# A gated cross-attention and expert-bias block on one core: the batch chain's scratch in PSUM, fewer VectorE operations in it, and mask rows loaded for two units by four transfers

## What is computed

```
x   = x + tanh(g_x) * attn(layernorm(x), ctx)          # x, ctx: (8, 512, 2048), fp32
attn(z, c), per window of 128 columns, 8 heads of 32:
      q = Wq z + bq;  k = Wk z + bk;  v = Wv c + bv    # 512 -> 256
      S = q^T k / sqrt(32), masked;  o = softmax(S) v
      out = (Wo gelu(o) + bo) * mask                   # 256 -> 512
x   = x + tanh(g_f) * ffn(layernorm(x))                # layernorm over the last axis (2048)
ffn(h): logits = h Wr^T + br (64 experts); s = softmax(logits); w = s kept at its 8 largest, else 0
      out = h * sum(w) + w @ expert_bias
```

## Time and profile before

| | |
|---|---|
| median of 3 runs | 1210.87 us (1206.91 to 1213.17) |
| the profiled execution | 1210.61 us, of which span 1208.5 us |
| granted TensorE clock | 0.985 of full speed |

### The profile page before, as it was taken

The page is one execution under the profiler, slowest core; times in us unless marked ns, Lnnn a source line. Parts: engine busy times, 40 slices in busy tenths (PEclk is TensorE's granted clock), DMA queues, the critical chain, the costliest instruction groups (busy, mean ns, idle before and its releaser), DMA issues.

```text
span 1208.5 us, 33324 instructions
## 1 busy us (share of the span) xinstructions
PE 1126.1 (93%) x11661; PEld 1046.1 (87%) x11661; DVE 975.5 (81%) x1882; ACT 1029.2 (85%) x3200; POOL 707.7 (59%) x660
## 2 busy tenths in 40 slices
PE   2699999989999899999999999999999989999977
PEld 2699999889988899898998999988998889989965
DVE  6658878988789777998779887898779977797757
ACT  4688999888989799988998889898998879998954
POOL 2366677466655577466764666746764647746621
PEclk9899999999999999999999999999999989999989
DMA  9267554775548844487556965478554884456433
GB/s 287 74 175 199 143 130 116 237 201 155 132 112 252 218 124 123 117 270 209 131 129 187 235 169 131 119 233 217 141 131 121 253 215 124 125 137 203 110 92 139
DMA packets 169766, 199.82 MB, mean 165 GB/s; under 512 B 27776, under 2 KB 104704, under 8 KB 169472
## 3 DMA queue, kind: packets, MB, share of 16 engines
q1 hardware_dynamic: 168448, 197.20, 59.8%
q10 hardware_dynamic: 1152, 0.50, 0.2%
HBM read 80.06 MB, written 33.65 MB: 94 GB/s over the span
## 4 chain that ended last, share of the span: by engine, by line
PE 56%; SPq 21%; DVE 10%; issue 4%; ACT 4%; DMA 3%; POOL 1%; DVEq 0%; ACTq 0%; POOLq 0%
SPq L521 13%; PE ring L310 7%; PE ring L312 7%; PE ring L311 7%; DVE X L900 4%; PE ring L366 4%; SPq L526 4%; PE ring L325 3%; PE ring L327 3%; PE ring L326 3%; PE ring L349 3%; PE ring L385 3%; PE ring L387 3%; PE ring L386 3%; PE ring L404 3%
## 5 line engine op out<-in xcount | busy, mean ns | idle before, releaser
L615 ACT ACTIVATE P<-ring,nmx 128x128 f32<-128x128 f32 x1024 | 358.6, 402 | 30.9 <-DVE nmx L766 30.3
L310 PE MATMUL ring<-z_hi,wqk_hi 128*128 128x256 f32 x1024 | 299.8, 293 | 24.3 <-DVE z_lo L965 22.0
L311 PE MATMUL ring<-z_hi,wqk_lo 128*128 128x256 f32 x1024 | 292.4, 286 | 0.0
L312 PE MATMUL ring<-z_lo,wqk_hi 128*128 128x256 f32 x1024 | 292.3, 285 | 0.0
L615 ACT ACTIVATION_READ_ACCUMULATOR P<-ring,nmx 128x1 f32 x1024 | 248.5, 243 | 0.0
L1058 POOL TENSOR_TENSOR z_lo<-z,z_hi 128x1024 fp32r<-128x1024 f32 x62 | 147.6, 2381 | 167.5 <-ACT z_hi L583 167.5
L310 PEld LDWEIGHTS ring<-z_hi,wqk_hi 128*128 128x128 f32 x1024 | 198.5, 194 | 37.2 <-DVE wqk_lo L940 21.9
L1070 POOL TENSOR_TENSOR X<-X,xt 128x512 f32<-128x512 f32 x128 | 165.5, 1293 | 67.7 <-DVE xt L801 67.6
L773 DVE STREAM_TRANSPOSE T<-P 128x512 f32<-128x512 f32 x256 | 169.2, 690 | 44.2 <-ACT P L615 24.0
L311 PEld LDWEIGHTS ring<-z_hi,wqk_lo 128*128 128x128 f32 x1024 | 198.9, 194 | 0.0
L312 PEld LDWEIGHTS ring<-z_lo,wqk_hi 128*128 128x128 f32 x1024 | 198.9, 194 | 0.0
(11 more groups left out here) (137 smaller groups left out, 2697.3 us busy)
## 6 DMA issues: line engine op xcount, KB each, us to landing
PT<-T SPq DMA_DIRECT2D x1018, 80.0 KB, 2.1
cx<-in_ctx SPq DMA_DIRECT2D x128, 256.0 KB, 3.9
out_y<-X SPq DMA_DIRECT2D x128, 256.0 KB, 3.1
X<-in_x SPq DMA_DIRECT2D x112, 256.0 KB, 4.6
mg<-in_mask SPq DMA_DIRECT2D x64, 128.0 KB, 3.2
X<-in_x SPq DMA_DIRECT2D x8, 512.0 KB, 8.5
sel<-rows_d SPq DMA_DIRECT2D x256, 3.0 KB
X<-in_eb SPq DMA_DIRECT2D x2, 512.0 KB, 7.7
```

The lines of the kernel that those rows point to most:

```text
L310: e.matmul(o, wqk_hi[:, t, cols], z_hi[:, t, :], t == 0, False)
L311: e.matmul(o, wqk_lo[:, t, cols], z_hi[:, t, :], False, False)
L312: last = e.matmul(o, wqk_hi[:, t, cols], z_lo[:, t, :], False, t == DT - 1)
L615: last = e.activation(P[:, n, :], bank("S", 4 * u + g)[:, k * W:(k + 1) * W], ACT.Exp, bias=nmx[u % 2][:, n:n + 1], accum_out=den[u % 2][: ...
```

## The change

- **Rows.** `load_rows(n)` serves units 2n and 2n+1 by four DMAs, 512 columns each, once; there are two buffers instead of three, and line 341 reads the unit's half twice by an access pattern whose middle step is 0. It is issued where the even unit's was, and waits for the same count of `s_pe`.
- **Batch chain.** The marks (`lr`), the masked exponentials and the sums live in the unused half of LT's PSUM bank (`low(b)`, `wsum`, `gain`); the bank is held until `ac_v` instead of `lg_v`. `c_gate` is gone. `c_scale` has a reduction, two `scalar_tensor_tensor` and a `tensor_scalar` instead of a reduction and three others.
- **Norms.** Adding EPS and negating the mean, before on DVE (823, 824, 926, 927), are on POOL before the power (EPS for norm2; EPS and the mean for the input norm); `norm2` waits for `ac_v` ahead of the aggregation.

```diff
-                take(("LT", b), t, C["c_top"] - C["LT"], lg_v, b + 1)
+                take(("LT", b), t, C["c_sc"] - C["LT"], ac_v, b + 1)
...
-                e.wait_ge(rows_in[u % NRW], 64 * (u // NRW + 1))
+                e.wait_ge(rows_in[u // 2 % NRW], 64 * (u // 2 // NRW + 1))
...
-                    e.matmul(bank("S", 4 * u + g)[:], ones3[head, :], sel[u % NRW][head, :, :].rearrange("p k i -> p (k i)"),
-                             True, False)
+                    e.matmul(bank("S", 4 * u + g)[:], ones3[head, :],
+                             sel[u // 2 % NRW][head, 2 * (u % 2):2 * (u % 2) + 2, :].rearrange("p w i -> p (w i)").unsqueeze(
+                                 1).to_broadcast([32, 2, U]), True, False)
...
-            def load_rows(u):
-                if u >= NRW:
-                    e.wait_ge(s_pe, u - NRW + 1)
+            def load_rows(n):
+                if n >= NRW:
+                    e.wait_ge(s_pe, 2 * (n - NRW + 1))
...
-                    e.dma_start(sel[u % NRW][32 * g + 12:32 * g + 15, :, :].rearrange("k (m w) i -> k m (w i)", m=2),
-                                rows_d[:, 2 * u:2 * u + 2, :].rearrange("k w i -> k (w i)").unsqueeze(1).to_broadcast(
-                                    [3, 2, U])).then_inc(rows_in[u % NRW], 16)
+                    e.dma_start(sel[n % NRW][32 * g + 12:32 * g + 15, :, :], rows_d[:, 4 * n:4 * n + 4, :]).then_inc(
+                        rows_in[n % NRW], 16)
...
-                for u in due(t, C["rows"]):
-                    load_rows(u)
+                for n in due(t, C["rows"], 32, TU // 2):
+                    load_rows(n)
...
             def norm2(b):
                 e.wait_ge(bn2_v, 16 * (b + 1))
+                if b:
+                    e.wait_ge(ac_v, b)
                 for t in range(DT):
                     e.bn_aggr(mv2[:, t, :], bn2[:, t, :, :].rearrange("p a c -> p (a c)")).then_inc(agg2_v, 1)
...
-                e.tensor_scalar(ln2[:, 0, :], mv2[:, :, 0], -1.0, None, ALU.mult).then_inc(neg2_v, 1)
-                e.tensor_scalar(ln2[:, 1, :], mv2[:, :, 1], EPS, None, ALU.add).then_inc(neg2_v, 1)
...
-                e.tensor_scalar(gate[:, 0, :], ln2[:, 2, :], cst[:, TF:TF + 1], None, ALU.mult).then_inc(dm_v, 1)
-                e.wait_ge(dm_v, b + 1)
-                e.tensor_tensor(gate[:, 1, :], gate[:, 0, :], ln2[:, 0, :], ALU.mult).then_inc(gate_v, 1)
...
-                    last = e.match_replace(lr[:, t, :], t8[:, t, :], lg[:, t, :], -3.0e38)
+                    last = e.match_replace(low(b)[:, t, :], t8[:, t, :], lg[:, t, :], -3.0e38)
...
-                e.tensor_tensor(lr[:], lr[:], lg[:], ALU.not_equal).then_inc(sel_v, 1)
+                e.tensor_tensor(low(b), low(b), lg[:], ALU.not_equal).then_inc(sel_v, 1)
+
+            def low(b):
+                return bank("LT", b)[:, DT * NX:2 * DT * NX].rearrange("p (t x) -> p t x", t=DT)
...
-                e.tensor_tensor(ex[:], ex[:], lr[:], ALU.mult).then_inc(wm_v, 1)
+                e.tensor_tensor(low(b), low(b), ex[:], ALU.mult).then_inc(wm_v, 1)
...
-                e.tensor_reduce(sc[:, :, 5:6], w2[:, :, 0, :], AX.X, ALU.add).then_inc(wm_v, 1)
-                e.wait_ge(gate_v, b + 1)
+                wsum, gain = bank("LT", b)[:, 0:DT], bank("LT", b)[:, DT:2 * DT]
+                e.tensor_reduce(wsum, w2[:, :, 0, :], AX.X, ALU.add).then_inc(wm_v, 1)
                 e.wait_ge(wm_v, 4 * b + 3)
-                e.tensor_tensor(sc[:, :, 4:5], sc[:, :, 5:6], gate[:, 0, :].unsqueeze(2), ALU.mult).then_inc(wm_v, 1)
-                e.tensor_tensor(sc[:, :, 7:8], sc[:, :, 5:6], gate[:, 1, :].unsqueeze(2), ALU.mult)
+                e.scalar_tensor_tensor(out=gain, in0=wsum, scalar=cst[:, TF:TF + 1], in1=rs2[:], op0=ALU.mult,
+                                       op1=ALU.mult).then_inc(wm_v, 1)
                 e.wait_ge(wm_v, 4 * b + 4)
-                e.tensor_scalar(sc[:, :, 6:7], sc[:, :, 4:5], 1.0, None, ALU.add).then_inc(ac_v, 1)
+                e.scalar_tensor_tensor(out=sc[:, :, 7], in0=gain, scalar=-1.0, in1=mv2[:, :, 0], op0=ALU.mult, op1=ALU.mult)
+                e.tensor_scalar(sc[:, :, 6], gain, 1.0, None, ALU.add).then_inc(ac_v, 1)
...
             def input_norm(b):
...
+                e.tensor_scalar(rs1[b % 2][:], mv[b % 2][:, :, 1], EPS, None, ALU.add).then_inc(eps1_g, 1)
+                e.tensor_scalar(nm1[b % 2][:], mv[b % 2][:, :, 0], -1.0, None, ALU.mult).then_inc(eps1_g, 1)
+                e.wait_ge(eps1_g, 2 * b + 2)
+                e.tensor_tensor(rs1[b % 2][:], rs1[b % 2][:], half[:], ALU.pow).then_inc(rstd1_g, 1)
```

More of the change, by code:

```diff
@@ L52 @@
     hT=37.5, hT_gap=0.25, ht_hi=41.25, ht_lo=41.75, R=47.25,
-    norm2=27.5, c_gate=33.5, L=36, LT=34, c_top=38.75, c_exp=37.75, c_w=40.75, c_sc=40.75, wT=43, wt_hi=43.25, wt_lo=42.25, mix=43.75, m_gap=0.25,
+    norm2=27.5, L=36, LT=34, c_top=38.75, c_exp=37.75, c_w=40.75, c_sc=40.75, wT=43, wt_hi=43.25, wt_lo=42.25, mix=43.75, m_gap=0.25,
     sx=44.75, sx_gap=1.25, x2=45.25, rl=48.5, rl_gap=2,
@@ L140, in gated_block_kernel @@
         bnst = sb("bnst", [128, DT, 4, 6])
-        mv = sb("mv", [128, DT, 2])
+        mv = [sb(f"mv{i}", [128, DT, 2]) for i in range(2)]
         bn2 = sb("bn2", [128, DT, 4, 6])
         mv2 = sb("mv2", [128, DT, 2])
-        ln1 = [sb(f"ln1_{i}", [128, 3, DT]) for i in range(2)]
-        ln2 = sb("ln2", [128, 3, DT])
+        rs1 = [sb(f"rs1_{i}", [128, DT]) for i in range(2)]
+        nm1 = [sb(f"nm1_{i}", [128, DT]) for i in range(2)]
+        rs2 = sb("rs2", [128, DT])
         L = sb("L", [128, D])
@@ L158, in gated_block_kernel @@
         tab = sb("tab", [128, 2])
-        gate = sb("gate", [128, 2, DT])
         acc = sb("acc", [128, 2])
@@ L196, in gated_block_kernel @@
         out_done = [[sem(f"out{t}{c}") for c in range(4)] for t in range(DT)]
[L197 removed]
+        bn1_v, agg1_v, eps1_g, rstd1_g = (sem(n) for n in ("bn1", "agg1", "eps1", "rstd1"))
         st_a = sem("st")
@@ L203, in gated_block_kernel @@
         gelu_a, othi_a, otlo_g, wo_pe, xt_v, x1_g = (sem(n) for n in ("gelu", "othi", "otlo", "WO", "xt", "x1"))
[L204 to L207 removed]
+        bn2_v, agg2_v, eps2_g, rstd2_g, ht_pe, hthi_a, htlo_v, r_pe = (sem(n) for n in (
+            "bn2", "agg2", "eps2", "rstd2", "hT", "hthi", "htlo", "R"))
+        l_a, lt_pe, lg_v, t8_v, neg_v, mr_v, sel_v, ex_a, w2_v, ac_v = (sem(n) for n in (
+            "L", "LT", "lg", "t8", "neg", "mr", "sel", "ex", "w2", "ac"))
         wm_v, wT_pe, wthi_a, wtlo_v, mix_pe, sx_a, x2_v = (sem(n) for n in (
@@ L1020, in _ @@
                         r_low(u, a)
-                for b in batch(t, C["c_gate"]):
-                    c_gate(b)
                 for b in batch(t, C["c_top"]):
```

56 lines of the change are left out of this document (18 added, 38 removed).

## The result

In the first comparison, four runs each, the changed kernel took 1196.45 us (1194.94 to 1200.85) against 1209.68 (1206.91 to 1213.17): a ratio of 0.9910, 95% interval 0.9883 to 0.9937. In a second one, nine runs against twenty, it was 1198.08 against 1209.15: 0.9924 (0.9896 to 0.9952). The ratios are estimated from all the runs and are not quotients of the medians (here 0.9908). So it is faster by 9 to 11 us. Forecast were 18.3 us and 1192.3; the time lies inside the range of 1186 to 1205, but the gain is little more than half of the forecast one.

What follows compares the result with a forecast made beforehand. TensorE was taken as the bound, losing time to waits and slow clock; 9.1 + 6.8 + 2.2 + 0.4 - 0.2 = 18.3 us off 1210.61 gave 1192.3, range 1188 to 1198, or 1186 to 1205 with two rivals.

Steps and rivals of the forecast that it cites:

- the price of PSUM: Five operations ahead of the division moved to PSUM: 0.3 us per chain or nothing, 0 to 2.1 in all, taken as nothing.
- the start: Kernel start, where nothing covers GpSimd's added small operations: a cost of 0 to 0.5 us, taken as 0.2.
- The chain on VectorE: Batch chain without the exposed waits behind GpSimd: 1.3 us gained in each of seven chains, 9.1 us.
- rival 2: ScalarE's evacuation is bound by TensorE's values, not the division: gain 2.1 us instead of 9.1, 1199.3 us; chance 0.10.
- The banks: New waits for permuted PSUM banks cost nothing if the chain moves, 0.6 us at most if it doesn't.
- rival 3: Row products reading the same columns twice with step 0 run slower: 0.6 us more per unit, 1230 us; chance 0.07.
- SP's queue: Earlier `PT<-T` start and fewer row loads let SP issue sooner in six stretches: TensorE gains 6.8 us.
- the clock: Shorter TensorE waits in the first two of the six batches avoid slow clock: 2.2 us gained.
- Rival 1: Transfers, not their issue, are late: the 6.8 us and most of the 2.2 stay away, 1201 us; chance 0.14.
- Rivals 4 and 5: 4: all `PT<-T` waits in the six stretches go, 1180, 0.07; 5: division's gain returns as waits behind it, 1208, 0.04.
- the prologue: One TensorE wait of 0.4 us in the prologue goes: 0.4 us gained.

Runs made afterwards that it cites:

- experiment 3: Changed kernel with the chain's scratch put back into SBUF, same operations: 1204.36 us against 1209.98 for the kernel before, ratio 0.9956.
- experiment 6: Changed kernel with eight 1024-column x loads, the four between the late `PT<-T` groups right behind the first: 1190.82 us against 1206.81 before the change, 0.9867.

## Why the prediction was right or wrong

The time fell into the range because the chain's half of the sum was right. Of the other half next to nothing came, and the forecast gain of 18.3 us was nearly twice the measured one. That even the forecast's own range, 1188 to 1198, reaches to the measured 1196.45 and 1198.08 is luck: it was widened for the price of PSUM and for the start, not for a queue that gives nothing back.

- **The chain on VectorE (9.1 us): right.** Measured 10.4 in the traces, 8.6 (5.5 to 11.6) as an experiment of its own. With all the change at 9 to 11, nothing clear of noise is left for the other terms. The steps of the chain hold one by one. The division comes 12.13 us behind the row product that begins the unit, 13.23 before: 1.10 sooner, 1.06 forecast. ScalarE's steps moved with it, so rival 2 is out: the first addition to x comes 18.93 behind the row product and not 20.30, gain 1.37 for 1.3, and it now waits for ScalarE's scaling, as foretold. That small SBUF operations stand behind GpSimd, read from the earlier trace rows, is shown by experiment 3.
- **The price of PSUM (0 to 2.1, taken as 0): right.** Five operations cost under 0.1 us per chain together. The 0.3 that the prediction worked out from the Trainium skill, page VectorE: DVE Perf Modes, section on the TRN2 errata, was a misreading too: the page's price is for a PSUM source, and of the five only the marks (862) read PSUM, the replacements write to it. Where the source did change, experiment 3 shows 0.02 us or less and not 0.06.
- **The banks: right, as long as the chain is short.** No wait for `ac_v` or for ScalarE's values in the changed kernel; with the scratch in SBUF the wait for `ac_v` is there, at 0.6, of which the hold itself costs 0.1.
- **Row products (rival 3, 1230): out.** Line 340's median is 384 ns, line 341's 385, and a steady unit is 15.92 us with both.
- **SP's queue (6.8 us) and the clock (2.2): wrong.** Of 9.0, 2.8 showed in the first trace and nothing in the second, which lost 3.2 us more than before; the row loads give 4.4 us alone and 0.6 (within 4.5) on top of the chain. The step that failed is "SP gains 1.06 because the first `PT<-T` group starts with the division, and 1.25 to 1.85 from the group of row loads: 2.3 to 2.9". The 1.06 is there (that group now starts 12.86 behind the row product, 13.97 before). The rest is the error of adding up an issue's duration as if it were its own: a row group's 1.25 to 1.85 of the earlier trace rows hardly came out of the queue: the issues behind it, the late `PT<-T` group's own among them, took longer, and SP came to wait for `cx_lo` on GpSimd ahead of a context load, a bound that the sum had not looked at. From the row product ahead of the chain to the second late group, SP gained 1.28 and 1.14 us in the two traces of the changed kernel (mean of six batches), hardly more than the 1.1 of the chain, and with the row loads alone 0.15; TensorE had gained 1.4 to 1.6. And what SP did gain ran into the landing, which the sum left out. The clock's 2.2 hung on shorter waits and went with them.
- **Rival 1 (1201, transfers and not issues are late): half right**, and it would have been the better forecast for this term: 0 instead of 9.0. The changed kernel lies between it and the forecast. Its sign was in the earlier trace rows, a landing of 4.43 us; I weighed it down with landings of 2.1 elsewhere, and those are the batches in which SP was late, two limits that the text treated as one or the other. The runs say that both happen, in one kernel, from batch to batch: the waits behind the earlier trace rows are draws and no fixed prices, as 16.9 and 19.2 us of one kernel show.
- **Rivals 4 and 5: out.** The waits didn't all go, and the chain's gain didn't come back as a wait behind the division.
- The start was forecast at -0.2 and the prologue at +0.4. The first row product is 0.04 later; a gain of 1.1 by the sixth unit is there, half of it lost again three units on.

What stays open: how much of the row loads' 4.4 us is left once the chain is shorter. The intervals allow 0 and 4. And why the row loads alone gave 4.4 us, when the queue got only 0.8 us shorter up to the second late group: in its one trace fewer landings are late, which the runs don't explain.

## What to carry to other kernels

Small VectorE operations that must run beside GpSimd do better in a PSUM bank that is free anyway: that was worth 1.06 us per chain in the traces here, more than twice what dropping operations was. A full DMA queue gives back little of what small issues leave, since the issues behind them take over a part. Fewer and larger loads that don't stand directly ahead of the transfers that an engine waits for brought some 7 us on top of the change (0.9867 beside 0.9924; 5 beside 0.9910), where halving the row loads brought nothing that could be measured on top; of the two, their number and their place, the times don't tell which did more. And before a load is put later, look up how long the longest group in its queue holds it: 14.75 slots of room looked like slack and were none. Read such sums of waits from more than one trace: 16.9 and 19.2 us are of the same kernel.

## What the runs showed of the hardware

- An issue of 128 x 1024 fp32 columns takes SP 0.40 us in the median (experiment 6), one of 128 x 512 takes 0.43 (the whole change), one of 128 x 32 takes 0.43 as well: the median issue doesn't go by bytes, landing does (6.1, 5.1 and 2.9 us).
- A mask load issued first behind a group of 16 `PT<-T` takes 0.58 us in the median where it otherwise takes 0.36, and up to 1.48 (the whole change, second trace); which load pays moves with the order.
- A VectorE operation of 256 elements with two SBUF inputs took 1.21 us when it started 0.35 us behind a GpSimd operation of 1.28, 0.43 us in the last chain with GpSimd idle, and 0.43 with one input in PSUM beside GpSimd.
- With x reduced to 32 columns the DMA engines are 0.19 busy from 248 to 252 us and 0.43 to 0.69 in the 16 us after, and TensorE still waits 1.5 us at 267: the last issue of the group ends 1.64 us before TensorE goes on, so SP's queue is what is late.
